# Six local-attention layers on one core: the engines' hand-written orders laid anew, with fewer and longer stretches of tiled matmuls and a second set of square tiles

## The reference

```python
for i in range(DEPTH):                                # 6
    x = attn_layer(shift_tokens(x), Wqkv[i], q_scale[i], k_scale[i], Wo[i]) + x
    x = ffn_layer(shift_tokens(x), ln_g[i], ln_b[i], W1[i], b1[i], W2[i], b2[i]) + x
...
def attn_layer(x, Wqkv, qs, ksc, Wo):                 # 16 heads of 64, windows of 32
    q, k, v = split(x @ Wqkv)
    q = l2norm(q) * qs;  k = l2norm(k) * ksc
    q = q * cos * scale + rotate_half(q) * sin * scale
    k = k * cos / scale + rotate_half(k) * sin / scale
    sim = einsum('bhwie,bhwje->bhwij', q, k of this and the last window) * 8    # masked
    out = einsum('bhwij,bhwje->bhwie', softmax(sim), v of this and the last window)
    return out @ Wo
```

## Time and profile before

| what | value |
|---|---|
| median of 3 runs | 3385.4 us |
| the profiled execution, its own time | 3384.84 us |
| span of its trace | 3383.0 us |
| busy share PE, DVE, ACT, POOL | 95%, 84%, 52%, 78% |
| granted TensorE clock, mean | 0.978 |
| packets of the queue that carries instructions (q8) | 318, 5.21 MB |

### The profile page before, as it was taken

One profiled execution on the slowest core, in us unless ns is written; L12 is line 12 of the kernel. 1 busy time (PEld: TensorE's weight loads), 2 busy tenths in 40 slices (PEclk: granted clock), 3 DMA queues, 4 the chain that ended last, 5 costly groups with the idle time before them and its releaser, 6 DMA issues.

```text
span 3383.0 us, 96906 instructions
## 1 busy us (share of the span) xinstructions
PE 3228.3 (95%) x39772; PEld 1496.3 (44%) x39772; DVE 2841.0 (84%) x3719; ACT 1766.0 (52%) x2636; POOL 2647.8 (78%) x1918
## 2 busy tenths in 40 slices
PE   6899976899999999999999999999999999999988
PEld 4333232444444444444444444444444444444443
DVE  6899936888888888888888888888888888888863
ACT  2578853455555555545555555555555555555542
POOL 3223217999899999999999989989989999888961
PEclk7899997999999999999999999999999999999999
DMA  7333122333333333333333333333333333333321
GB/s 215 83 62 65 39 95 70 84 79 80 86 84 92 85 79 78 94 77 92 84 80 86 84 90 86 80 81 89 81 90 85 80 86 82 90 84 79 79 64 53
DMA packets 200487, 283.38 MB, mean 84 GB/s; under 512 B 56561, under 2 KB 82417, under 8 KB 199153
## 3 DMA queue, kind: packets, MB, share of 16 engines
q1 hardware_dynamic: 196304, 262.75, 31.6%
q10 hardware_dynamic: 3744, 14.43, 1.2%
HBM read 44.30 MB, written 19.55 MB: 19 GB/s over the span
## 4 chain that ended last, share of the span: by engine, by line
PE 78%; SPq 2%; POOL 2%; DVE 1%; issue 1%; DMA 1%; ACT 1%; DVEq 0%; POOLq 0%
PE ly_pj_ps L1005 20%; PE ly_to_ps L1081 20%; PE ly_pair_ps L1069 11%; PE ly_pair_ps L1049 9%; PE ly_to_ps L1111 4%; PE ly_pair_ps L1099 4%; PE ly_pair_ps L1103 3%; PE ly_nq_ps L1015 3%; PE ly_pair_ps L1036 2%; SPq L914 1%; PE ly_pair_ps L1089 1%; PE ly_pair_ps L1058 1%; SPq L904 1%; PE ly_pair_ps L1029 1%; DMA ly_kp<-ly_kr 0%
## 5 line engine op out<-in xcount | busy, mean ns | idle before, releaser
L1206 DVE SCALAR_TENSOR_TENSOR ly_prod<-ly_pj_ps,ly_few,ly_tables 128x1024 f32<-128x1024 f32 x768 | 964.9, 1272 | 149.4 <-ACT ly_sq L1403 132.2
L1005 PE MATMUL ly_pj_ps<-ly_xs,ly_wqk 128*128 128x512 f32 x1536 | 802.0, 625 | 30.6 <-DVE ly_prod L1206 14.8
L1081 PE MATMUL ly_to_ps<-ly_u,ly_mvo 128*128 128x512 f32 x1536 | 763.8, 606 | 0.9 <-issue 0.7
L1403 ACT ACTIVATE ly_sq<-ly_pj_ps 128x512 f32<-128x512 f32 x768 | 451.4, 603 | 574.7 <-PE ly_pj_ps L1005 494.1
L1499 POOL TENSOR_TENSOR ly_sq<-ly_sq 128x512 f32<-128x512 f32 x384 | 488.1, 1278 | 119.1 <-ACT ly_sq L1403 118.2
L1503 POOL TENSOR_TENSOR ly_sx<-ly_sx,ly_smax 128x1024 f32<-128x1024 f32 x192 | 365.7, 1905 | 126.0 <-DVE ly_smax L1282 125.5
L1434 ACT COPY ly_u<-ly_pair_ps 128x1024 f32<-128x1024 f32 x384 | 369.4, 1013 | 133.0 <-PE ly_pair_ps L1069 133.0
L1005 PEld LDWEIGHTS ly_pj_ps<-ly_xs,ly_wqk 128*128 128x128 f32 x1536 | 266.8, 192 | 347.7 <-issue 236.9
L1049 PEld LDWEIGHTS ly_pair_ps<-ly_kp,ly_qp 64*32 64x32 f32 x24576 | 277.4, 106 | 281.3 <-issue 242.6
L1081 PEld LDWEIGHTS ly_to_ps<-ly_u,ly_mvo 128*128 128x128 f32 x1536 | 272.6, 190 | 276.2 <-issue 262.9
L1069 PE MATMUL ly_pair_ps<-ly_pt,ly_xt 32*128 32x512 f32 x3072 | 385.3, 615 | 9.5 <-ACT ly_u L1434 6.8
(11 more groups left out here) (125 smaller groups left out, 4232.4 us busy)
## 6 DMA issues: line engine op xcount, KB each, us to landing
ly_qp<-ly_qr SPq DMA_DIRECT2D x1536, 64.0 KB
ly_kp<-ly_kr SPq DMA_DIRECT2D x1536, 64.0 KB, 2.0
ly_xt<-ly_xt SPq DMA_DIRECT2D x48, 192.0 KB
ga_parts_dram<-ga_parts SPq DMA_DIRECT2D x16, 384.0 KB, 2.4
ga_qs<-ga_parts_dram SPq DMA_DIRECT2D x96, 64.0 KB
ga_ks<-ga_parts_dram SPq DMA_DIRECT2D x96, 64.0 KB
ly_wqk<-in_wqk SPq DMA_DIRECT2D x24, 256.0 KB, 3.8
ly_mvo<-mvo_dram SPq DMA_DIRECT2D x24, 256.0 KB, 3.8
```

Of the source, the lines that this page charges most:

```text
L1005: pe.matmul(pj_ps[:, j % 2, :], wqk[:, g, j % TILES, :], xs[:, n % 2, WIN:], start=True, stop=True).then_inc(proj_ready.sem, 1)
L1081: last = pe.matmul(to_ps[:], mvo[:, 4 * (h // 4) + BESIDE[h % 4], :], u[:, :, :, h, :].rearrange("p t c q -> p (t c) q"), start=(h == 0), ...
L1206: dve.scalar_tensor_tensor(prod[:, k], pj_ps[:, j % 2, :].unsqueeze(1).to_broadcast([P, 2, N]), gains[:, n // B, k:k + 1], tables[:, table ...
L1403: act.activation(sq[:, k, :], pj_ps[:, j % 2, :], ACT.Square).then_inc(sq_done.sem, 1)
```

## The change

The functions that compute stay as they are but for one: `sq` gets a second set of four tiles. Group g uses set g % 2, and `squares` waits for the square sums two groups back, not one. All five `body` lists are written anew. The number of steps of each kind in an item is the same, and so is the number of instructions of the built program: 1,539 an item on PE, in both (matmuls, weight loads, and 34 that only wait).

```diff
-        sq = sb("sq", [P, TILES, N])
+        sq = sb("sq", [P, 2, TILES, N])
...
-                    if k == 0 and UNITS * n + g:
-                        act.wait_ge(ns_ready.sem, UNITS * n + g)
-                    act.activation(sq[:, k, :], pj_ps[:, j % 2, :], ACT.Square).then_inc(sq_done.sem, 1)
+                    if k == 0 and UNITS * n + g >= 2:
+                        act.wait_ge(ns_ready.sem, UNITS * n + g - 1)
+                    act.activation(sq[:, g % 2, k, :], pj_ps[:, j % 2, :], ACT.Square).then_inc(sq_done.sem, 1)
...
-                    pool.tensor_tensor(sq[:, 2 * (k % 2)], sq[:, 2 * (k % 2)], sq[:, 2 * (k % 2) + 1], ALU.add).then_inc(sq_added.sem, 1)
+                    side, at = k // 2 % 2, 2 * (k % 2)
+                    pool.tensor_tensor(sq[:, side, at], sq[:, side, at], sq[:, side, at + 1], ALU.add).then_inc(sq_added.sem, 1)
...
-                if x_4 is not None: scores(x_4, 0, 0)
-                if x_3 is not None: project(x_3, 4)
-                if x_4 is not None: scores(x_4, 0, 1)
...
+                if x_4 is not None: scores(x_4, 0, 0); scores(x_4, 0, 1); scores(x_4, 1, 0); scores(x_4, 1, 1)
```

More of the change, by code:

```diff
@@ L1176, in body @@
-                if x_4 is not None: spread_norms(x_4, 3)
-                if x_7 is not None: down(x_7, 1)
-                if i == ITEMS + 6: turn_back(6)
-                if x_3 is not None: project(x_3, 9)
-                if x_5 is not None: attend(x_5, 1)
-                if x_3 is not None: project(x_3, 10, 11)
+                if x_5 is not None: attend(x_5, 1)
+                if x_3 is not None: project(x_3, 8, 9)
+                if x_7 is not None: up_gate(x_7, 2)
+                if i == ITEMS + 6: turn_back(6)
@@ L1182, in body @@
+                if x_6 is not None: turn_ffn_tokens(x_6)
+                if x_7 is not None: up_value(x_7, 2); down(x_7, 1)
+                if x_3 is not None: project(x_3, 10)
+                if x_5 is not None: attend(x_5, 2)
+                if x_3 is not None: square_sums(x_3, 1); project(x_3, 11, 12)
+                if x_5 is not None: attend(x_5, 3)
+                if x_3 is not None: project(x_3, 13)
                 if x_7 is not None: down(x_7, 2)
-                if x_5 is not None: attend(x_5, 2)
@@ L1184, in body @@
-                if x_3 is not None: square_sums(x_3, 2); project(x_3, 12, 13)
-                if x_5 is not None: attend(x_5, 3)
-                if x_3 is not None: project(x_3, 14)
                 if i == ITEMS + 5: turn_back(0, 1)
@@ L1349, in body @@
                 if x_7 is not None: normalise(x_7)
+                if x_5 is not None: prob_sums(x_5, 2); inverse_sums(x_5, 2)
+                if i == ITEMS + 6: add_sums(2)
                 if x_3 is not None: products(x_3, 1)
+                if x_4 is not None: scale_keys(x_4, 1)
+                if x_5 is not None: prob_sums(x_5, 3); prob_blocks(x_5, 2); inverse_sums(x_5, 3)
+                if x_3 is not None: products(x_3, 2)
+                if x_7 is not None: gated(x_7, 0)
+                if x_3 is not None: products(x_3, 3)
@@ L1351, in body @@
+                if x_7 is not None: gated(x_7, 1)
+                if x_4 is not None: scale_keys(x_4, 2)
                 if i == ITEMS + 6: add_sums(3)
-                if x_4 is not None: scale_keys(x_4, 1)
-                if x_5 is not None: prob_sums(x_5, 3); inverse_sums(x_5, 3); prob_blocks(x_5, 2)
-                if x_7 is not None: gated(x_7, 0)
-                if x_3 is not None: products(x_3, 2)
                 if x_5 is not None: prob_blocks(x_5, 3)
-                if x_7 is not None: gated(x_7, 1)
@@ L1358, in body @@
-                if x_3 is not None: products(x_3, 3)
-                if x_4 is not None: mask_scores(x_4, 0)
+                if x_4 is not None: mask_scores(x_4, 0); mask_scores(x_4, 1); score_maxima(x_4, 0)
+                if x_3 is not None: products(x_3, 4, 5)
+                if x_6 is not None: attention_sum(x_6)
+                if x_4 is not None: scale_keys(x_4, 3)
+                if x_3 is not None: products(x_3, 6, 7)
                 if i == ITEMS + 6: add_sums(4)
-                if x_4 is not None: score_maxima(x_4, 0)
@@ L1376, in body @@
-                if x_3 is not None: products(x_3, 12)
+                if x_4 is not None: mask_scores(x_4, 2); score_maxima(x_4, 2)
+                if x_3 is not None: products(x_3, 14, 15)
             bodies(body)
@@ L1462, in body @@
-                if x_3 is not None: squares(x_3, 0)
-                if x_4 is not None: widen_norms(x_4, 0)
-                if x_3 is not None: squares(x_3, 1)
+                if x_4 is not None: copy_sums(x_4)
+                if x_3 is not None: squares(x_3, 0, 1)
                 if x_5 is not None: copy_tokens(x_5)
-                if x_4 is not None: widen_norms(x_4, 1)
+                if x_4 is not None: widen_norms(x_4, 0); widen_norms(x_4, 1)
+                if x_5 is not None: exponentials(x_5, 2); exponentials(x_5, 3)
```

161 lines of the change are left out of this document (72 added, 89 removed).

## The result

The kernel after takes 3413.5 us (median of 4 runs, 3412.0 to 3422.5) against 3384.6 us before (4 runs beside them): 1.0088 times as long, 95% interval 1.0067 to 1.0109. The forecast was 3420 us, within 3340 to 3475, with slower as the likelier side. The sign, the size and the main cause came out as told; several terms inside the sum did not.

What follows compares the result with a forecast made beforehand. The prediction took PE's own sum of work to bound the kernel, and summed 3384.8 - 98 + 101 + 30 + 12 - 10 = 3420 us, 1.0% slower, range 3340 to 3475 us.

Steps and rivals of the forecast that it cites:

- What bounds it: PE's own sum of work is the layers' time; changes in PE's row count one to one until POOL at 52.45 us.
- the row of four: Four halves of scores in a row, 512 instructions: PE stops for the next instruction block in every item, +101 us.
- Fewer switches: Tiled stretches on PE go from 15 to 7 an item; with three joins 2.1 us an item, -98 us.
- three joins give 0.6 us: In the row of four halves of scores, each join saves 0.19 us, 0.6 us together.
- Scores, square sums, scores: At groups 2 and 3, 288 instructions in 2.15 us nearly fill a block in some 27 items: +30 us.
- The block behind the row of four: Last scores, two combines, attend: its instruction fetch may be held back by data transfers, 0 to 50 us, taken as +12.
- The waits of before: PE's earlier waits, 5.6 us on issue (counted in other terms) and 5.3 us on late keys, may go: -10 us.
- Rival C: Data transfers slow the fetch at the row of four, 3500 us, or DVE's 0.7 us of slack is gone, 3467; 13%.
- DVE's slack at attend 1: DVE frees the slot for attend 1 with 0.7 us left: taken as 0, up to +1 us an item (+47).
- A: Instruction fetch is hidden, two or more blocks stand ready, the row of four costs nothing: 3277 us; 15%.
- B: The fetch takes only 2.8 us, so gains and stops nearly cancel: 3368 us, or up to 3395; 24%.
- D: The switches have no effect, because a switch hides something else: 3420 + 98; under 1%.

Runs made afterwards that it cites:

- e5: The kernel after with groups 0 and 1 scored by half as many matmuls of 64 weight columns instead of 32, changing part of the results: 3270.1 us.
- e3: The kernel after with its row of four halves of scores split in two rows of two, combine 13 and project 5 between: 3382.2 us.
- e8: Like e6, but three whole matmuls (combine 12, combine 13, project 5) between the two rows of scores: 3369.7 us.
- e9: Like e6, but combine 13 ahead of the first row of scores, and project 4 and 5 between the rows: 3368.0 us.
- e10: Like e9, with combine 14 between project 4 and 5 as well, so three whole matmuls between the rows: 3372.6 us.
- e7: Like e6, but project 5 and combine 14 between the two rows of scores, in place of combine 13 and project 5: 3350.3 us.
- e6: e3 with one swap on DVE, gated 1 ahead of products 3: 3344.1 us.

## Why the prediction was right, and where it wasn't

**What bounds it.** Right for the kernel before and for the change: PE's own time made it, and in e5 the row of four lost 3.0 us and the item 3.1. DVE stands close behind it. In e3, e8, e9 and e10 the stops shrank by 79 to 86 us and the kernel took only 31 to 46 us less, since PE then waited for DVE, 45 to 69 us against 13 in the kernel after.

**Fewer switches, -98 us.** The 0.20 us at each stretch is confirmed, 8 x 0.20 = 1.6 us an item. The step that failed is "a half in mid-row should take 0.59 us", so "three joins give 0.6 us". I had taken the starts of the weight loads of a half alone as its pace in a row. A row of two in e8 takes 1.52 us with no stop in it; two halves alone take 2 x 0.79 = 1.58. A join is worth 0.06 us, not 0.19, three of them 0.2. In the row of four 170 weight loads take 1.95 us, which is 0.73 for 64. The term is (1.6 + 0.2) x 46.5 = -84 us at most; the sum of the steps without stops, by my count, went from 57.5 to 55.8 us an item, which makes it -79.

**The row of four, +101 us.** Right in its cause and near in its sum: 90.0 us of stops from 600 to 3200 us, 91.6 in the whole program by the page's group of L1049, which is 86 more than before. Each side of the subtraction was low. The fetch was put at 3.3 us against 1.2 us of work in a block. With the pace above, a block of 256 scores' instructions holds 0.73 x 2 = 1.5 us, and the stop is 87.5 / 45 = 1.9 us, so a block takes 3.4 us from entry to use. Counted directly, from PE's first instruction of the block inside the row to its first of the next, it is 3.57 us on the mean of the 45, from 2.90 to 4.38: 1.10 to the packet's start, 1.11 for the packet, 1.35 from its landing to PE. The forecast had 0.7 + 1.2 + 1.4, so what it put too low is the time to the packet's start. The two errors cancel, so the right sum was in part luck; e5 and e3 show that its cause was not. The Trainium skill, "Runtime: NRT & Kernel Launch", Instruction fetch mechanics, calls the crossing of such a block "mostly hidden", because an engine dispatches more slowly than the stream fills; before, the trace agrees (5.6 us in 45 items), and in a row of small tiled matmuls it doesn't: 1.9 us stay open in every item.

**"Scores, square sums, scores", +30 us.** Oversized: in my count the groups 2 and 3 with their transposes lose 0.17 us an item, 7 us in all. The step that failed is "work of 2.0 to 2.4 against 3.0 to 3.4" wherever a block is nearly filled by such a place. The trace shows items 11 to 23 with the border inside group 3 and without any stop: where a border falls early in a half, the packet of queue 8 goes out 0.5 to 1.7 us before PE executes the border's instruction (items 11 to 22), so the request runs ahead of the matmuls, and blocks of 1.83 to 2.08 us pass without a stop. In the row of four no packet runs ahead: they leave 0.6 to 2.1 us behind the border, even where it lies 23 instructions deep (item 45). Why the two places differ wasn't tried.

**The block behind the row of four, +12 us.** As fetch, about 0: PE's waits on "issue" name the combines nowhere. But the two combines take 2.17 us on the mean instead of 1.91, 0.26 more an item and 12 us in all, for a reason of which I had not thought, below. Right number, wrong cause: luck. The reading of the earlier trace rows behind this term, that data transfers fill the queues and so hold the packet back, isn't borne out either. By a count in both traces, the packets that leave more than 3 us behind their border (70 before, 61 after) find the 16 engines 28% and 36% busy with data in that time, those that leave 0.3 to 2 us behind it 37% and 39%. What does set the long lags is open.

**The waits of before, -10 us.** Half right: the keys' 5.3 us went, the 5.6 us are part of the stops.

**Rival C's kind, small.** DVE's slack at attend 1 held: the wait for that slot is `PE ly_pair_ps L1069 <- DVE ly_kr L1261: 1.2, 2, 0.6` after, and 1.2 us in two waits before as well. But I had looked at that one place only. Projections now wait 10.3 us for products, where the earlier trace rows has no such line.

**Sum again,** by what was measured, for 46.5 items: -79 (steps without stops), +86 (stops on issue), +12 (slow combines), +10 (products), -5 (keys) give +24 us; measured are +28 to +29. Some of the rest is in the row of four: its mean of 5.07 us less 1.96 of stop is 3.1, and the four halves at 0.73 are 2.9.

**The rivals.** A (the fetch hidden, 3277 us) falls by the row of four, and B by the sign. D is out by the item's steps. e5 comes at 3270 us, near rival A's 3277, but by chance: it takes away some 0.85 us an item of work besides the stop. With that work back (46.5 x 0.85 = 40 us) a kernel after without its stops would take some 3310 us; this is an estimate from e5, and no run has it.

## What to carry to other kernels

Count instructions, not only microseconds: where PE's row packs 256 of them into much less than the 3.6 us that a block took here, as small tiled matmuls do with 1.5 us for 256, it can stop at the end of a block. This is a sign and no sharp limit: blocks of 1.83 us passed without a stop where the packet had left early, and blocks of 5.3 to 6.6 us ended in a stop of 0.2 to 0.8 us, in six of the 12 of the earlier trace rows, where it left 3.0 to 3.7 us late. Two or three whole matmul steps between such rows (e3, e8) brought the stops from 2.0 us an item to 0.1 to 0.25. Then look at what the moved work asks of others: each of e3, e7, e8, e9 and e10 cut the stops and then waited for DVE, on a slot, a mask or a product that had had just enough time. And a join of two like stretches is worth the switch outside it only as far as a row without stops shows it: here 0.06 us, not 0.19.

## What the runs showed of the hardware that I had not expected

The granted clock of TensorE fell behind some of the stops. The item at 2234 us, PE's timeline and then two windows (PE busy and count, clock, DMA share, GB/s):

```profile
2234.27 1.51 PE L1049 MATMUL ly_pair_ps<-ly_kp,ly_qp 64*32 64x64 f32 x125
2237.60 1.21 PE L1049 MATMUL ly_pair_ps<-ly_kp,ly_qp 64*32 64x64 f32 x92 [1.81 <-issue]
2238.74 3.65 PE L1081 MATMUL ly_to_ps<-ly_u,ly_mvo 128*128 128x512 f32 x4
2242.32 1.57 PE L1069 MATMUL ly_pair_ps<-ly_pt,ly_xt 32*128 32x512 f32 x12
...
2232.00:2237.40 5.40, 3.78 (x172) 1.00 0.39 103
2240.00:2242.00 2.00, 2.00 (x3) 0.50 0.31 74
```

Ahead of the two combines the clock is 1.00 (2.4 GHz), in them 0.50 (1.2 GHz), and they take 2242.32 - 2238.74 = 3.58 us instead of 1.91. Eight such drops stand between 700 and 3200 us of the kernel after, near 720, 1073, 1247, 1421, 1889, 2240, 2475 and 2950 us, each behind a stop of 1.7 to 2.7 us; before, the clock stays at 1.00 from 662 to 3266 us, and in e3 and e6, whose stops are short, as well. The cause of the stop doesn't matter: e8 and e10, with 3.9 us of fetch stops, show three drops between 700 and 3200 us, behind idle times of 1.97, 1.87 and 2.10 us in which PE waited for DVE. One of them in e8, PE's timeline and two windows:

```profile
2200.11 1.13 PE L1005 MATMUL ly_pj_ps<-ly_xs,ly_wqk 128*128 128x512 f32 x2 [1.87 <-DVE ly_prod L1198]
...
2196.00:2200.00 4.00, 2.24 (x6) 1.00 0.45 108
2201.50:2203.50 2.00, 2.00 (x126) 0.50 0.58 152
```

So what goes ahead of a drop is PE standing still for some 2 us. Why only eight of some 44 such stops were followed by one is open; the length doesn't decide it, as a stop of 2.51 us at 2004 us was not.

The other surprise is how long the stream's packet takes: 0.92, 1.50 and 1.59 us for 16 KB in three places, next to data on the same 16 engines, and then 1.2 to 1.6 us from landing to PE's next instruction, in each of the 45 stops in the row of four.
